# Attention and mixture-of-experts kernel: plan of the next tiles in each batch's first group, the finish of a batch on VectorE and the transposes of its rows two to three steps sooner

## What is computed

```python
x = x + layernorm(attention(layernorm(x)))      # float16, 8 batches of 512 rows
x = x + layernorm(experts(layernorm(x)))

def experts(x, Ws, bs, Wg, Wu, Wd):             # 256 -> 688 -> 256, 8 experts
    logits = xt @ Ws + bs
    topk_w, topk_idx = top_k(logits, 2)
    topk_w = softmax(topk_w)
    combine = sum(one_hot(topk_idx, 8) * topk_w[..., None], axis=1)
    h = silu(xt @ Wg[e]) * (xt @ Wu[e])         # for each expert e
    y = h @ Wd[e]
    return sum over e of y * combine
```

## Time and profile before

| | before |
|---|---|
| median of 3 runs | 888.35 us |
| lowest, highest | 885.34, 891.23 us |
| the profiled execution | 890.5 us |
| its span in the profile | 888.7 us |
| TensorE busy | 718.2 us (81%) |
| VectorE busy | 635.0 us (71%) |
| ScalarE busy | 536.3 us (60%) |
| GpSimd busy | 434.0 us (49%) |

### The profile page before, as it was taken

One profiled execution on the slowest core, in us unless ns is written; L12 is line 12 of the kernel. 1 busy time (PEld: TensorE's weight loads), 2 busy tenths in 40 slices (PEclk: granted clock), 3 DMA queues, 4 the chain that ended last, 5 costly groups with the idle time before them and its releaser, 6 DMA issues. The chain is left out here.

```text
span 888.7 us, 22060 instructions
## 1 busy us (share of the span) xinstructions
PE 718.2 (81%) x6822; PEld 471.2 (53%) x6823; DVE 635.0 (71%) x2034; ACT 536.3 (60%) x1086; POOL 434.0 (49%) x515
## 2 busy tenths in 40 slices
PE   3476787778788899979998998889885999999930
PEld 1144444445443355545554564567773878778720
DVE  5777898889877988887897778467551556556545
ACT  4688875867656676756765674665642444344427
POOL 3563432644534556774675467577352233242228
PEclk9889997989985799999988997899996999999975
DMA  6435232463332101221112111223335233233248
GB/s 192 136 118 153 82 113 71 126 194 116 112 130 63 43 14 26 50 48 26 26 28 53 19 32 34 41 40 57 50 86 137 37 44 46 36 47 42 30 113 291
DMA packets 72812, 68.91 MB, mean 78 GB/s; under 512 B 6800, under 2 KB 66320, under 8 KB 72720
## 3 DMA queue, kind: packets, MB, share of 16 engines
q1 hardware_dynamic: 59440, 53.23, 19.7%
q0 software_dynamic: 13280, 14.49, 11.6%
HBM read 34.04 MB, written 31.29 MB: 74 GB/s over the span
## 5 line engine op out<-in xcount | busy, mean ns | idle before, releaser
L944 ACT ACTIVATE pT<-bank 128x512 f16<-128x512 f32 (+1 forms) x384 | 200.3, 534 | 100.1 <-PE bank L1521 98.7
L728 POOL TENSOR_SCALAR_AFFINE_SELECT pT<-pT 128x512 f16<-128x512 f16 x128 | 88.2, 734 | 144.7 <-ACT pT L944 144.4
L1087 DVE TENSOR_REDUCE nmax<-bank 128x1 f16<-128x384 f32 (+2 forms) x216 | 126.1, 597 | 34.7 <-PE bank L1510 33.3
L1944 POOL DMA_INDIRECT expert_rows<-y_sb,dest x36 | 56.0, 1554 | 120.1 <-DVE y_sb L2063 114.6
L1100 DVE CUSTOM_DVE_ANT_0 unused<-bank,mask 128x384 f16<-128x384 f32 (+2 forms) x224 | 103.6, 483 | 14.4 <-PE bank L1499 12.8
L2138 PE MATMUL bank<-xT,gu_part 128*128 128x256 f16 (+1 forms) x792 | 95.9, 280 | 2.6 <-issue 1.7
L1614 PE MATMUL bank<-tile_xT,gu_part 128*128 128x256 f16 (+1 forms) x616 | 90.9, 289 | 8.5 <-DVE stage L1284 8.4
L2138 PEld LDWEIGHTS bank<-xT,gu_part 128*128 (+1 forms) x792 | 78.5, 102 | 19.0 <-issue 4.2
L1552 PEld LDWEIGHTS bank<-va,pT 128*128 128x128 f16 x1280 | 55.4, 99 | 51.1 <-issue 27.8
L1552 PE MATMUL bank<-va,pT 128*128 128x17 f16 x1280 | 68.0, 174 | 15.8 <-POOL pT L728 15.8
L162 POOL DMA_INDIRECT dispatch_rows<-rows,slot x64 | 66.9, 1046 | 21.5 <-issue 16.7
(11 more groups left out here) (218 smaller groups left out, 1618.6 us busy)
## 6 DMA issues: line engine op xcount, KB each, us to landing
expert_rows<-tile_in SPq DMA_DIRECT2D x8, 1024.0 KB, 6.2
stage<-wg SPq DMA_DIRECT2D x8, 688.0 KB, 4.2
stage<-wu SPq DMA_DIRECT2D x8, 688.0 KB, 4.2
stage<-wd SPq DMA_DIRECT2D x8, 640.0 KB, 4.3
gu_part<-expert_rows SPq DMA_DIRECT2D x16, 256.0 KB, 5.7
out<-gu_part SPq DMA_DIRECT2D x16, 256.0 KB, 2.9
tile_in<-dispatch_rows SPq DMA_DIRECT2D x21, 130.0 KB, 2.2
rows<-dispatch_rows SPq DMA_DIRECT2D x18, 130.0 KB, 2.2
```

The lines of the kernel that those rows point to most:

```text
L728: last = gp.affine_select(out=diagonal, in_=diagonal, compare_op=ALU.is_ge, fill=0.0, base=0, pattern=[[0, J], [1, P]], channel_multiplier=-1)
L944: sc.activation(pT[:, lo:hi], ST_BANK[i % 2][:, 0:hi - lo], ACT.Exp, scale=1.0 / INV_SCALE).then_inc(p_ready, 1)
L1087: v.tensor_reduce(columns, S_BANK[i % 2][:, 0:n * len(heads)].rearrange("p (j n) -> p j n", n=n), AX.X, ALU.max, negate=True).then_inc(s_m ...
```

## The change

Three tables and the time of one eviction change. The plan goes from group 1 to group 0 of each batch, at the same steps. In the finish, the scaling of y goes from (2, 1) and (2, 2) to (1, 10) and (1, 11), what follows it by two steps each, and the scaling of the rows from (2, 9) and (2, 10) to (2, 6) and (2, 7). The transposes "xn2T" go from step 11 to step 9 of group 2, and ScalarE's taking of them from step 12 or 11 to step 10 or 9. GpSimd's and SyncE's programs are the same.

```diff
                     {"q": (1, 2), "k": (3, 4), "v": (5,), "max": (6, 7), "y0": (0,), "y1": (2,)},
-                    {"q": (1, 2), "k": (3, 4), "v": (5,), "max": (6, 7), "xn2T": (11,)},
+                    {"q": (1, 2), "k": (3, 4), "v": (5,), "max": (6, 7), "xn2T": (9,)},
...
-                   {"q": (1,), "k": (3,), "v": (5,), "max": (7,), "xn2T": (11,)},
+                   {"q": (1,), "k": (3,), "v": (5,), "max": (7,), "xn2T": (9,)},
...
-            return grp * NF + {"q": 3, "k": 5, "v": 7, "max": 8, "attT": 9, "xnT": 11, "y0": 1, "y1": 3, "xn2T": 12}[what]
+            return grp * NF + {"q": 3, "k": 5, "v": 7, "max": 8, "attT": 9, "xnT": 11, "y0": 1, "y1": 3, "xn2T": 10}[what]
...
-        AT_FINISH = ((1, 4), (1, 5), (1, 6), (1, 7), (2, 1), (2, 2), (2, 3), (2, 4), (2, 5), (2, 6), (2, 9), (2, 10))
-        AT_PLAN = ((1, 8), (1, 9), (1, 10), (1, 11))
+        AT_FINISH = ((1, 4), (1, 5), (1, 6), (1, 7), (1, 10), (1, 11), (2, 1), (2, 2), (2, 3), (2, 4), (2, 6), (2, 7))
+        AT_PLAN = ((0, 8), (0, 9), (0, 10), (0, 11))
```

## The result

| | before | changed |
|---|---|---|
| median | 887.90 us (4 runs) | 915.03 us (4 runs) |
| lowest, highest | 885.34, 891.23 us | 913.30, 918.63 us |
| the profiled execution's span | 888.7 us | 912.5 us |

The changed kernel takes 1.0282 times the time of the one before (95% interval 1.0243 to 1.0321), 27 us more. From the first exp of a batch to that of the next, batches 1 to 3 took 166.6 us before and 166.7 after, batch 4 75.5 and 77.8, batches 5 to 7 together 248.4 and 272.0. So nearly all of it lies in batches 5 to 7. What follows the attention phase was 2 us shorter, and the span grew by 23.8.

A forecast was written before the change was run, and what follows sets the result against it. In batches 5 to 7 TensorE was taken as nearly full, with GpSimd's queue making rstd late. Terms 8.1 + 7.8 + 3.0 - 2.5 summed to +16.4 us, from the median 888.35 to 905, range 892 to 915.

The forecast's parts named there:

- What bounds, and who sets rstd: Batches 5 to 7: TensorE close to full; GpSimd's queue, not the moments, makes the roots and so rstd late.
- The y scale: Steps (1, 10) and (1, 11), batches 5 to 7: the scale waits for rstd; +8.1 us (4.5 to 8.1).
- the blocked case: In (1, 10): GpSimd's cuts hold the y scale to their end, at 380.8 instead of 379.6 without blocking.
- The rows' scale: Steps (2, 6) and (2, 7), batches 5 to 7: new rstd wait, part given back at group's end; +7.8 us (4 to 9).
- The plan in group 0: Steps (0, 8) to (0, 11): costs 0 to 1.7 us a batch, taken as 1.0 in batches 5 to 7; +3.0.
- the last piece: The plan's last 1.7 us in group 0, standing before maxima and gate of the next group; earlier pieces fill gaps.
- Batches 1 to 4: Roots there wait for moments, so both come sooner and waits for cut and rows go; -2.5 us (-6 to 0).
- Removing L1252's stall from (1, 9) wins nothing.: Group 1, step 9: no gain, since TensorE waited for the cut until 374.91 anyway, 1.95 us.
- The clock rival: Batches 5 to 7: new waits lower TensorE's clock, adding 5 to 9 us, to 910 to 914; chance 0.14 (over 910).
- The sum: Whole kernel: 8.1 + 7.8 + 3.0 - 2.5 = +16.4 us, giving 905; chance 0.62 for 898 to 910.
- The signs: Batches 5 to 7: L1068 idle 3 to 5 us, (2, 11) wait gone, GpSimd's waits for moments not shrinking.
- Faster, 871: Rstd there when VectorE comes, before 374 and 391 in batch 5: tail waits go, some 17 us; chance 0.06.

The follow-up runs named there:

- the run with the root first: The changed kernel with GpSimd's root of (2, 0) moved ahead of the store of the tile: 898.10 us, 1.0093 of the kernel before.
- the run with the scatters alone: The kernel before with only the scatters of (1, 0) moved to (1, 1), behind cut and root, in batches 5 to 7: 890.96 us, 1.0005.

## Why the prediction was right, and by how much its steps were off

The direction and the mechanism were right, and 915 is at the top of the range of 892 to 915; the forecast of 905 was 10 us short. I set the prediction's terms against the lengths of steps, from one exp to the next, summed over batches 5 to 7.

- **What bounds, and who sets rstd.** Right, and shown by changing GpSimd's order alone: one root ahead of the store gives 17 us of the 25 to 27 back, both roots all of it.
- **The y scale, forecast +8.1.** Steps (1, 10) to (2, 1) grew by 4.3, 2.5 and 3.0: 9.8. Of that TensorE's idle time is 6.8 and its longer busy time 2.9. VectorE waited 5.37 us, about as forecast, but the first half of the scale took 1.22, between the 0.6 without blocking and the 1.9 of the blocked case that I took. Missing from the sum is the clock, most of all in batch 5: there TensorE was busy 9.1 us instead of 5.9 in these steps, and eight matmuls behind the wait took 1.89 us instead of 1.17 in the earlier trace rows. The granted clock is 0.50 there from 379.75 on, already behind the wait for the cut, where it was 1.00 before (from 374.9); why it fell at that point the traces don't say. Undoing it gave 7 to 8.
- **The rows' scale, forecast +7.8.** Steps (2, 6) to (2, 11) grew by 3.4, 2.8 and 4.1: 10.3, and undoing it gave 15. TensorE's wait came out near the forecast (4.42 us in batch 5 against 4.7), partly by luck, since two errors offset each other: VectorE waited 5.76 us for rstd where I had 4.7, and the scale took 1.13 us where I had it blocked for 1.8. The two halves of this scale had been slow already, 1.52 and 1.28 us before (from 396.50 and 398.55) against 1.13 and 0.60 now, so the blocking was no new cost of this part. The tail gave back 3.3 in batch 5, more than the 2.3 that I had counted. Mis-sized was what follows the wait. In the run with the root first, (2, 8) takes 1.57 us and (2, 9) 1.71; in the changed kernel 7.03 and 2.81. That is 6.6 us for a wait of 4.42: the other 2.1 are TensorE at the lower clock level, busy 5.4 us instead of 3.3 for the same 42 matmuls. Over the three batches TensorE's idle time is 7.0 of the 10.3 and its longer busy time 3.2. Undoing the part gives more than its steps grew, since it doesn't lead back to the kernel before: with the scale of y sooner and the rows' scale at its old place, the same steps take 3.5 us less than before, and TensorE is idle 6.2 us in them instead of 9.3. That is 13.7 us of the difference; the little that is left isn't settled.
- **The plan in group 0, forecast +3.0.** The most mis-sized term. Group 0 grew by 1.3, 2.5 and 1.3, and the step after it, (1, 0), by 1.3, 0.2 and 0.8: 7.4 together, and undoing it gave 7. TensorE's idle time is 5.2 of the 7.4. I had priced the last piece only and let the others lie in gaps. That the plan's instructions are stalled by GpSimd's cut stood in my own, and I used that row to price the scale but not the plan. In batch 4, said to be untouched, step (0, 11) grew from 2.0 to 3.0.
- **Batches 1 to 4, forecast -2.5.** The gain didn't come: batches 1 to 3 together +0.1, batch 4 +2.3. The 2.3 may be chance, since batch 4 unchanged took from 75.5 to 79.2 us in different executions. The waits for the cut and for the rows went as said, but VectorE waits 1.54 us for rstd, the scale beside the cut takes 1.14, not 0.6, and the maxima queue behind both. I hadn't carried the stall over from the late batches to the early ones.
- **"Removing L1252's stall from (1, 9) wins nothing."** Right: in the changed kernel it takes 0.16 us, and TensorE waits 1.96 us for the cut as before. The run with the scatters alone shows the other side: without that wait a stall there costs as much.
- **The clock rival, 910 to 914.** It came true in size, and the sum had nothing for it. The mean granted clock over batches 5 to 7 fell from 0.92 to 0.90, and TensorE was busy 5.2 us longer: half of the 10 us that the forecast was short. But it was wrong about where: group 3 of batches 5 to 7 became shorter, by 0.9, 2.5 and 0.6 us, as the waits that had stood just ahead of it had moved back by three steps, and the low level with them (TensorE is busy 4.1 us less in these groups, and idle as long as before).
- **The sum.** 7.4 + 9.8 + 10.3 - 4.0 (group 3) = 23.5 of the 23.6 us of batches 5 to 7; the steps left out, (1, 1) to (1, 9) and (2, 2) to (2, 5), nearly cancel. The signs: L1068 idle 5 to 7 us instead of the 3 to 5 named, no wait of the transposes, GpSimd's waits for moments in that stretch unchanged (11.3 us, 2 times, in both).
- **Faster, 871.** It was to decide at rstd before 374 and 391. With both roots moved it is 0.5% faster, not 2%. Two things were longer than I had counted: the plan's part (in that run's profile group 0 and step (1, 0) of batches 5 to 7 are 12.2 us longer than before), and the early batches, of which I had counted on 10 us and got none.

The Trainium skill ("SBUF — State Buffer", Who interferes with whom) says that a VectorE instruction with two inputs in SBUF contends with a GpSimd instruction that reads SBUF, and that the one that issues first shuts the other out for its whole length. The traces agree that VectorE is held: 2.18, 2.42 and 3.02 us for plan instructions of 8 to 32 elements, each ending with GpSimd's low part. They don't bear out that the first to issue wins: the records of the 2.42 and of the 3.02 begin 0.04 and 0.03 us ahead of GpSimd's cut (373.59 and 373.63, 374.23 and 374.26), and VectorE was the one held. GpSimd was still on a DMA at both moments (until 373.62 and 374.82), so who issued first can't be read from these records. These are instructions with two inputs, so the 2.42 us that the prediction set beside the rule for two-port modes belongs to this rule. For a two-port mode only the scale can speak, which has one tensor as its input: 1.13 to 1.22 us where it takes 0.60 alone, and each of its two instructions ends 0.08 or 0.09 us behind one of GpSimd's. I had weighed the blocking for the scale alone.

## What to carry to other kernels

Before an operation is put sooner, find what makes its last input, and read what stands ahead of that on its in-order engine: here it was the producer that had to move, and moving it alone was worth 17 us. A wait added in a loop of full engines can cost more than its length, here 6.6 us for 4.42, since TensorE comes out of it at its lower clock. And if short VectorE instructions stand beside GpSimd's long ones, ask whether TensorE waits for the same GpSimd instruction anyway: that cover is what makes the stall free, and it is lost as soon as either of the two moves.

## What the runs showed of the hardware that I had not expected

- A VectorE instruction can be held over several GpSimd instructions in a row: 3.02 us for eight elements, over the two instructions of a cut and a low part, in the run with the scatters alone. GpSimd isn't slowed by it, though the records look so. Cut and low part show 1.80 and 1.73 us where the cut comes straight behind the store's DMA, with the plan beside them (354.22 in the changed kernel) or without (352.19 in the kernel before, 1.80 and 1.74), and 1.23 and 1.15 us elsewhere, with the held L1252 beside them (373.63 before) or without (378.45 in the changed kernel, 1.23 and 1.16). From the end of the DMA ahead to the end of the low part it is 2.35 us in either case (354.78 to 357.13, 373.62 to 375.97).
- After a wait of 4.42 us TensorE stayed at the lower level for over 4 us of work: eight matmuls took 1.89 us instead of 1.03, the transposes behind them 1.01 instead of 0.62. The first root that came in time (the run with the root first) took this away together with the wait.
